# CIN tower with a top MLP: a correction tile over all partitions, top layers by batch halves in three rounded passes, and an earlier first step

## What is computed

```
z   = einsum('bhd,bmd->bhmd', h, x0).reshape(batch, H * M, dim)
out = relu(einsum('bcd,oc->bod', z, W[i]) + b[i])      # i = 0: h = x0;  i = 1: h = the first 64 rows of out
feat = sum over dim of (out0[:, 64:], out1)            # 192 values per sample
h = max([feat, dense_ctx] @ W_top1 + b_top1, 0)        # 208 -> 512
h = max(h @ W_top2 + b_top2, 0)                        # 512 -> 256
y = h @ W_top3
```

## Time and profile before

| | us |
|---|---|
| median of 3 runs (lowest, highest) | 1989.1 (1988.71, 1989.22) |
| profiled execution, its own time | 1987.74 |
| its span | 1985.9 |
| PE busy | 1947.4 (98%) |
| DVE busy | 1912.4 (96%) |
| POOL busy | 1802.8 (91%) |
| ACT busy | 1710.7 (86%) |

### The profile page before, as it was taken

The page is one execution under the profiler, slowest core; times in us unless marked ns, Lnnn a source line. Parts: engine busy times, 40 slices in busy tenths (PEclk is TensorE's granted clock), DMA queues, the critical chain, the costliest instruction groups (busy, mean ns, idle before and its releaser), DMA issues.

```text
span 1985.9 us, 28534 instructions
## 1 busy us (share of the span) xinstructions
PE 1947.4 (98%) x7176; PEld 1340.1 (67%) x7176; DVE 1912.4 (96%) x1231; ACT 1710.7 (86%) x1943; POOL 1802.8 (91%) x708
## 2 busy tenths in 40 slices
PE   3999999999999999999999999999999999999998
PEld 1767766766766766766766666666666666666664
DVE  5999999999999999999999999999999999999991
ACT  4989888888888888888888888888888888888883
POOL 5999999999999999999999999999999999999881
PEclk9999999999999999999999999999999999999999
DMA  8987777777777777777777777777777777777720
GB/s 224 236 203 191 193 182 191 194 184 188 193 185 187 194 186 186 194 187 185 194 188 184 194 189 182 194 190 182 194 191 181 195 192 179 195 192 179 192 63 1
DMA packets 268641, 364.14 MB, mean 183 GB/s; under 512 B 107713, under 2 KB 108097, under 8 KB 268498
## 3 DMA queue, kind: packets, MB, share of 16 engines
q1 hardware_dynamic: 256946, 351.56, 71.9%
q0 software_dynamic: 8192, 8.40, 1.8%
q10 hardware_dynamic: 3488, 4.00, 0.7%
HBM read 347.02 MB, written 16.78 MB: 183 GB/s over the span
## 4 chain that ended last, share of the span: by engine, by line
PE 92%; POOL 5%; issue 2%; DMA 1%; ACT 1%; ACTq 0%; DVE 0%; POOLq 0%
PE out L718 60%; PE out L700 21%; PE out L708 8%; POOL zl L269 5%; PE out L702 1%; PE out L765 0%; PE hrep L765 0%; POOL emb L245 0%; DMA emb<-in_tables,idx 0%; DMA xrep<-fields_dram 0%; DMA fields_dram<-emb 0%; ACT hrep L445 0%; PE out L758 0%; PE z L758 0%; PE hrep L758 0%
## 5 line engine op out<-in xcount | busy, mean ns | idle before, releaser
L269 POOL TENSOR_TENSOR zl<-prod,zh 128x2048 fp32r<-128x2048 f32 (+2 forms) x384 | 1545.6, 4056 | 72.4 <-ACT zh L432 72.4
L718 PE MATMUL out<-zh,w1h 128*128 128x512 f32 x1856 | 754.6, 407 | 1.5 <-ACT relu L438 0.8
L718 PE MATMUL out<-zl,w1h 128*128 128x512 f32 x1856 | 724.4, 390 | 0.0
L718 PE MATMUL out<-zh,w1l 128*128 128x512 f32 x1856 | 723.3, 390 | 0.0
L432 ACT ACTIVATE zh<-prod 128x2048 fp32r<-128x2048 f32 (+2 forms) x384 | 652.7, 1700 | 70.0 <-DVE prod L639 45.3
L445 ACT ACTIVATE hrep<-out,b_sb 32x512 f32<-32x512 f32 (+1 forms) x768 | 495.1, 645 | 84.8 <-PE out L702 75.0
L700 PE MATMUL out<-prod,w_sb 128*128 128x512 f32 x1024 | 464.0, 596 | 31.1 <-DVE prod L574 26.1
L718 PEld LDWEIGHTS out<-zh,w1h 128*128 128x128 f32 x1856 | 348.2, 188 | 170.7 <-POOL zl L269 62.9
L718 PEld LDWEIGHTS out<-zl,w1h 128*128 128x128 f32 x1856 | 348.3, 188 | 75.9
L718 PEld LDWEIGHTS out<-zh,w1l 128*128 128x128 f32 x1856 | 348.8, 188 | 74.5 <-issue 2.6
L700 PEld LDWEIGHTS out<-prod,w_sb 128*128 128x128 f32 x1024 | 194.8, 190 | 228.0 <-issue 218.2
(11 more groups left out here) (64 smaller groups left out, 701.6 us busy)
## 6 DMA issues: line engine op xcount, KB each, us to landing
rot_low<-fields_dram SPq DMA_DIRECT2D x512, 256.0 KB, 6.3
rot_high<-fields_dram SPq DMA_DIRECT2D x512, 256.0 KB, 4.3
xrep<-fields_dram SPq DMA_DIRECT2D x252, 128.0 KB, 2.7
left_y<-fields_dram SPq DMA_DIRECT2D x256, 64.0 KB, 2.2
fields_dram<-emb SPq DMA_DIRECT2D x504, 32.0 KB, 4.6
left_x<-fields_dram SPq DMA_DIRECT2D x252, 64.0 KB, 2.3
emb<-in_tables,idx POOLq DMA_INDIRECT x256, 4.4
w_sb<-in_w ACTq DMA_DIRECT2D x1, 1024.0 KB, 5.2
```

The lines of the kernel that those rows point to most:

```text
L269: pool.tensor_tensor(zl[u][:, 0:size, :], product[:, 0:size, :], zh[u][:, 0:size, :].bitcast(F32), ALU.subtract).then_inc(zl_made[u], 1)
L718: mm = nc.tensor.matmul(out1[:, :], w[:, k, :], z[:, t, :], start=start and t == 0 and part == 0, stop=stop and t == size - 1 and part == 2)
```

## The change

1. **Left part.** A new tile `left_high` has zeros on partitions 0 to 63 (written once). `round_left` rounds only partitions 64 to 127 into it, and `left_low` computes `left_parts = lz - left_high` over all 128 partitions, no longer in place. `round_left` waits for the `left_low` before and no longer for PE; `left_low` now waits for PE (`l0_done`). PE's matmul is the same. In the steps with b = 0, `copy_left` stands behind the rounding of groups 0 and 3 on ACT, and no longer ahead of it.
2. **Top layers.** The order is by batch half, then by tile. Weights, features and the first layer's outputs are split in a rounded part (ACT) and a remainder (DVE), and each fp32 matmul of layers 1 and 2 becomes three fp32r matmuls (`in_three`). The first half's work needs only blocks 0 to 31, so its preparation stands ahead of the last step's results. Layer 2 waits for its inputs tile by tile. Layer 3 stays in fp32. The remainders lie in tiles that the steps no longer use; `w0b_sb` moves into `prod[3]`.
3. **Prologue.** ACT now writes both groups of block 0's second half (SP wrote one), and issues the load of `w1_sb` ahead of its first write. `copy_x(0, 0)`, the second half of `xrep` and `copy_left(0)` stand ahead of the wait for block 1's rows on ACT, and `load_low(1, 1)` ahead of it on SP.

The core of the diff (semaphores and some copies of the same pattern are left out):

```diff
+        left_high = sb("left_high", [P, SC], F32R)
         left_parts = sb("left_parts", [P, SC], F32R)
...
-        w0b_sb = sb("w0b_sb", [P, LOW, OUT])
+        w0b_sb = prod[3][:, 0, :].rearrange("p (a b) -> p a b", b=OUT)
...
+        wt1_parts = [rot_low[0][:, 2 * p:2 * p + 2, :].bitcast(F32R) for p in range(2)]
+        wt2_parts = [rot_low[1][:, 2 * p:2 * p + 2, :].rearrange("p a (b c) -> p (a b) c", c=H2).bitcast(F32R)
+                     for p in range(2)]
+        feat_parts = [(zh[3 + half], zl[3 + half]) for half in range(MN)]
+        h1_parts = [(zh[half], zl[half]) for half in range(MN)]
+        h1_sb = prod[:MN]
+        h2_sb = prod[2:2 + MN]
...
-        banks = [t[:, :] for t in (out0, out1, hrep[0], hrep[1], xr, lz)] + [z4[:, 0, :], z4[:, 1, :]]
+        banks = [t[:, :] for t in (xr, lz, hrep[0], hrep[1])] + [z4[:, 0, :], z4[:, 1, :], out0[:, :], out1[:, :]]
...
+        def sums_relu1(half):
+            first = 1 + half * (BLOCKS // MN)
+            return sums[:, first:first + BLOCKS // MN, SROWS:ENTRY]
...
             write_first(sp, 0, 0, first_written)
-            sp.wait_ge(gathered[0], GATHERED_APART)
-            write_first(sp, 1, 0, scratch_written[0])
             sp.wait_ge(first_written, WRITTEN_APART)
             load_low(0, 0)
             sp.wait_ge(scratch_written[0], written(0, 1))
             load_left(sp, 0, left_y, LEFT, left_y_loaded)
+            load_low(1, 1)
             sp.wait_ge(gathered[1], 16 * GATHERS)
             write_groups(sp, 1, 1, (0, 1))
-            load_low(1, 1)
             load_high(0, 0)
...
             def round_left(n):
                 act.wait_ge(left_made, n + 1)
                 if not known(n) or n > 0:
-                    act.wait_ge(l0_done, n * 2)
-                act.activation(left_parts[:, :], lz[:, :], ACT.Copy).then_inc(left_rounded, 1)
+                    act.wait_ge(left_split, n)
+                act.activation(left_high[HID:P, :], lz[HID:P, :], ACT.Copy).then_inc(left_rounded, 1)
...
                 if not first and is_up_to(i, c, LAST - 2):
                     copy_x(m + 2, b)
+                round_split(m, 0, in_parts(0, b), p1_made, prod[1])
+                round_split(m, 3, in_parts(3, b), z4_made[0], z4)
                 if not first and b == 0 and is_up_to(i, c, LAST - 2):
                     copy_left(i * 2 + (c + 2) // 2)
-                round_split(m, 0, in_parts(0, b), p1_made, prod[1])
-                round_split(m, 3, in_parts(3, b), z4_made[0], z4)
                 if is_past(i, c, 0):
                     finish_l1(m - 1, 1 - b, i * 2 + (c + 1) // 2 - 1)
...
+            act.wait_ge(first_gathered[0], 16)
+            act.dma_start(w1_sb[:, :, :], w1).then_inc(w1_loaded, 16)
             act.wait_ge(first_gathered[1], 16)
             write_first(act, 0, 1, first_written)
-            act.dma_start(w1_sb[:, :, :], w1).then_inc(w1_loaded, 16)
             act.wait_ge(gathered[0], GATHERED_APART)
-            write_first(act, 1, 1, scratch_written[0])
+            for g in range(HGATHERS):
+                write_first(act, 1, g, scratch_written[0])
             act.wait_ge(first_written, WRITTEN_APART)
             load_first_xrep(act, 0, first_xrep_loaded)
             act.wait_ge(scratch_written[0], written(0, 1))
             load_left(act, 0, left_x, 0, left_x_loaded)
+            load_first_xrep(act, 1, xrep_loaded)
+            copy_x(0, 0)
+            copy_left(0)
             act.wait_ge(gathered[1], 16 * GATHERS)
             write_groups(act, 1, 1, (2, 3))
-            copy_x(0, 0)
-            load_first_xrep(act, 1, xrep_loaded)
-            copy_left(0)
             round_left(0)
...
+            def fill_feat0(half):
+                to = feat0[HID:P, half * SC:(half + 1) * SC].rearrange("p (m b r) -> p b m r", b=HALVES, r=SROWS)
+                for b in range(HALVES):
+                    first = half * (BLOCKS // MN) + b
+                    act.activation(to[:, b], sums[b * HID:(b + 1) * HID, first:first + BLOCKS // MN, 0:SROWS],
+                                   ACT.Copy).then_inc(feat0_made, 1)
+            def round_feat0(half):
+                act.wait_ge(feat0_made, (half + 1) * HALVES)
+                act.wait_ge(split_used[3 + half], STEPS)
+                act.activation(feat_parts[half][0][:, 0, :], feat0[:, half * SC:(half + 1) * SC],
+                               ACT.Copy).then_inc(feat_rounded, 1)
+            def round_sums(half):
+                act.activation(feat_parts[half][0][:, 1, :].rearrange("p (n r) -> p n r", r=ROWS), sums_relu1(half),
+                               ACT.Copy).then_inc(feat_rounded, 1)
+            act.wait_ge(top_loaded, 96)
+            act.wait_ge(sums_made, BLOCKS // MN + 1)
+            fill_feat0(0)
+            act.activation(wt1_parts[0], wt1_sb[:, :, :], ACT.Copy).then_inc(wt_rounded, 1)
+            round_feat0(0)
+            round_sums(0)
+            act.activation(wt2_parts[0], wt2_sb[:, :, :], ACT.Copy).then_inc(wt_rounded, 1)
             act.wait_ge(sums_made, BLOCKS + 1)
-            to = feat0[HID:P, :].rearrange("p (m b r) -> p b m r", b=HALVES, r=SROWS)
-            for b in range(HALVES):
+            fill_feat0(1)
             finish_l1(LAST, 1, BLOCKS - 1)
+            round_feat0(1)
...
+            def h1(j):
+                half, c = j // C1, j % C1
                 act.wait_ge(h1_done, j + 1)
-                act.activation(h1_sb[c][:, half, :], banks[j], ACT.Relu, bias=bt1_sb[:, c:c + 1]).then_inc(h1_made, 1)
+                act.activation(h1_sb[half][:, c, :], banks[j], ACT.Relu, bias=bt1_sb[:, c:c + 1]).then_inc(h1_made, 1)
+            def round_h1(j):
+                half, c = j // C1, j % C1
+                act.wait_ge(h1_made, j + 1)
+                if c == 0:
+                    act.wait_ge(split_used[half], STEPS)
+                act.activation(h1_parts[half][0][:, c, :], h1_sb[half][:, c, :], ACT.Copy).then_inc(h1_rounded, 1)
+            h1(0)
+            act.wait_ge(sums_made, BLOCKS + 2)
+            round_sums(1)
+            for j in range(1, C1 * MN):
+                h1(j)
+                round_h1(j - 1)
+            round_h1(C1 * MN - 1)
...
             def left_low(n):
                 dve.wait_ge(left_rounded, n + 1)
-                nc.vector.tensor_tensor(left_parts[HID:P, :], lz[HID:P, :], left_parts[HID:P, :].bitcast(F32),
+                if known(n) and n == 0:
+                    dve.wait_ge(left_zeroed, 1)
+                else:
+                    dve.wait_ge(l0_done, n * 2)
+                nc.vector.tensor_tensor(left_parts[:, :], lz[:, :], left_high[:, :].bitcast(F32),
                                         ALU.subtract).then_inc(left_split, 1)
...
+            def low_weights(k, wt, parts):
+                dve.wait_ge(wt_rounded, k + 1)
+                nc.vector.tensor_tensor(parts[1], wt[:, :, :], parts[0].bitcast(F32), ALU.subtract).then_inc(wt_split, 1)
...
+            def low_h1(j):
+                half, c = j // C1, j % C1
+                high, low = h1_parts[half]
+                dve.wait_ge(h1_rounded, j + 1)
+                nc.vector.tensor_tensor(low[:, c, :], h1_sb[half][:, c, :], high[:, c, :].bitcast(F32),
+                                        ALU.subtract).then_inc(h1_split, 1)
...
+            low_weights(0, wt1_sb, wt1_parts)
+            low_feat0(0)
+            low_sums(0)
+            low_weights(1, wt2_sb, wt2_parts)
             dve.wait_ge(relu1_made, STEPS)
             sum_rows(BLOCKS, slice(0, P), slice(1, 1 + HALVES))
+            low_feat0(1)
+            low_sums(1)
+            for j in range(C1 * MN):
+                low_h1(j)
...
+            def in_three(out, w, z, first, last):
+                for part, (wp, zp) in enumerate(((w[0], z[0]), (w[1], z[0]), (w[0], z[1]))):
+                    mm = nc.tensor.matmul(out, wp, zp, start=first and part == 0, stop=last and part == 2)
+                return mm
...
+            pe.wait_ge(wt_split, 1)
+            for half in range(MN):
+                pe.wait_ge(feat_split, 2 * (half + 1))
+                for c in range(C1):
+                    j = half * C1 + c
+                    if banks[j] is out1:
+                        pe.wait_ge(relu1_made, STEPS)
+                    for k in range(2):
+                        mm = in_three(banks[j], [w[:, k, c * P:(c + 1) * P] for w in wt1_parts],
+                                      [z[:, k, :] for z in feat_parts[half]], k == 0, k == 1)
                     mm.then_inc(h1_done, 1)
-            pe.wait_ge(h1_made, C1 * MN)
-            for c in range(C2):
-                for half in range(MN):
+            pe.wait_ge(wt_split, 2)
+            for half in range(MN):
+                for c in range(C2):
+                    j = half * C2 + c
                     for k in range(C1):
-                        mm = nc.tensor.matmul(banks[c * MN + half], wt2_sb[:, k, c * P:(c + 1) * P],
```

(17 more changed lines are left out.)

31 lines of the change are left out of this document (19 added, 12 removed).

## The result

| us | before | after |
|---|---|---|
| median (lowest, highest), 4 runs each, same chip | 1989.02 (1988.71, 1989.22) | 1972.51 (1972.13, 1972.92) |
| profiled execution: its own time, its span | 1987.74, 1985.9 | 1972.53, 1970.7 |

The ratio is 0.9916, with a 95% interval of [0.9903, 0.9928]: 16.5 us faster. The forecast was 1970.5, so the result is 2.0 us above it and inside the range of 1966 to 1978.

What follows compares the result with a forecast made beforehand. DVE was taken to bound the kernel from about 270 us, hidden behind PE's 98% busy. Gains 6.9 + 9.85 + 0.4 + 1.5 = 18.65 cut the span from 1985.9 to 1967.3, giving a median of 1970.5; range 1966 to 1978.

Steps and rivals of the forecast that it cites:

- Part 1, forecast 6.9: Left part in the steady steps: 57 pairs fall to PE's 29.734 us each, gaining 6.9 us; bounds 0 and 9.7.
- the chain's two paces: PE's pairs of steps: 29.734 us each up to 242.56 us, PE's own need; 29.867 from 272.38, set by DVE.
- the three held intervals: DVE starts around `left_low`, once a pair: 0.11, 0.12 and 0.14 us too long, together 0.37, all closed by the change.
- the cut at PE's own pace: DVE would need 29.50 us a pair, but PE needs 29.734, so the gain is only 0.133 a pair.
- The rival that DVE stays the bound: Steady steps: the intervals have another cause and stay; gain only 11.3 us, 1977.8 in all; chance 0.11.
- `copy_left`, forecast 0: ACT, steps with b = 0: moving it behind two roundings costs 0, hidden by a 0.6 us margin before POOL needs `zh`.
- The rival that rounding would be late for POOL: `copy_left` delays `zh` of group 1; each 0.1 us beyond the margin costs 6.3, with 0.4 more 1996; chance 0.04.
- Part 2, forecast 9.85: Top layers: three passes at 0.229 us a matmul without PE waits, 25.59 us against 35.44; bounds 7 to 10.
- Three passes bring nothing: Top layers: matmuls on reused tiles run at fp32's 0.446 us; layers 1 and 2 take 21.4 each, total 1991; chance 0.02.
- The last step, forecast 0.4: Last step, where PE waits for POOL: DVE's lead lets POOL start earlier, gaining 0.4 us; bounds 0 and 0.7.
- Part 3, forecast +1.5: Prologue: first copy at 21.1 us, first `hrep` at 30.9 instead of 32.38, gaining 1.5; bounds -0.5 and 3.0.
- the prologue gives back: Prologue: writes and loads collide, first `hrep` no earlier, 1972.0; chance 0.09 for prologue or top layers falling short.

Runs made afterwards that it cites:

- run 5: The kernel before with one line changed: `left_low` in place on partitions 0 to 127, output not the reference's; 1980.93 us, ratio 0.9961.
- run 6: The kernel before with one line changed: `left_low` in place on partitions 0 to 63, output not the reference's; 1982.34 us, ratio 0.9964.
- run 1: The kernel before with only the left part changed, including the place of `copy_left`; 1981.13 us, ratio 0.9959.
- run 12: The changed kernel with `copy_left` back ahead of the rounding of groups 0 and 3 in steps with b = 0; 1974.04 us, ratio 0.9922.
- run 4: The changed kernel with the prologue of before; 1971.09 us, ratio 0.9909 to before.
- run 9: The changed kernel with block 0's second-half writes shared by SP and ACT again and the `w1_sb` load back behind the first write; 1969.47 us, ratio 0.9899.
- run 11: The changed kernel with SP's 1 MB `load_low(0, 0)` issued behind its wait for block 0's written rows; 1971.90 us, ratio 0.9912.
- run 7: The changed kernel with only the load of `w1_sb` put back behind the first write; 1973.92 us, ratio 0.9925.
- run 10: run 9 with the load of `w1_sb` issued only behind the second half of `xrep`; 1971.52 us, ratio 0.9909 to before.
- run 3: The kernel before with only the prologue changed; 1993.06 us, ratio 1.0018.
- run 2: The kernel before with only the top layers changed; 1979.32 us, ratio 0.9948.

## Why the prediction came out as it did

**Part 1, forecast 6.9, measured 6.56.** The reading of the chain's two paces, the bound on DVE, the three held intervals and the cut at PE's own pace were right. Runs 5 and 6 settle the cause. PE's own pace was taken as 29.734 and is 29.740, which makes 0.3 over 57 pairs. The rival that DVE stays the bound fell in run 1. One of the signs named was wrong: DVE's idle time of 0.11 us in the pair doesn't show as a wait of DVE; what shows are waits of ACT for PE.

**`copy_left`, forecast 0.** Right for the margin in the steady state, which is what was argued, and wrong as a sum: the first steps, where its rows land late, weren't looked at. The move is worth 1.2 us there (run 12). The rival that rounding would be late for POOL did not occur; the margin of 0.6 held.

**Part 2, forecast 9.85, measured 10.12** (25.32 us against 25.59 forecast). The pace of 0.229 us for a matmul holds on the reused tiles (it is 0.227: 96 of them in 21.76 us, 1943.15 to 1964.91), and PE doesn't wait once. ACT's preparations are eight instructions, as in the sum, though the list of the change counts seven; they were done at 1939.8, and the last relu waited 3.36 us for PE. Layer 3's own part is 3.56 in place of 3.63. "Three passes bring nothing" fell.

**The last step, forecast 0.4, measured 0.38, for another reason.** Between the last group and the last step lie four more pairs, 118.96 us against 119.54, a gain of 0.58 which the forecast hadn't counted. The last step alone got 0.16 longer (24.93 against 24.77, from layer 0's last matmul to the end of the split matmuls). So DVE's lead was worth nothing there.

**Part 3, forecast +1.5, measured -1.84.** This is the step that failed, beyond its bound of -0.5 (by run 4 and after, -1.6), and the sign that was named for it, a first copy after 22 us, came: 24.98. What stands behind the time of block 0's rows was right: in run 9, with the rows at 15.93, the first copy came at 21.37 (forecast 21.1) and the first `hrep` at 30.03 (30.9). The wrong step was the sentence that ACT's two more writes come first, "but `w1_sb` starts earlier and is out of their way", which put the rows at 16.3 with 17.2 as the bound; they were written at 19.97. Three things were missed in it:
- The early load of `w1_sb` is not out of the way but in the way of the gather ahead: 2.5 us.
- Taking a write from SP moves forward all that SP issues next. That is 1 MB, and it got ahead of the writes (3.2 us of the 5.2, run 11). Only `left_x` was looked at for that, not the writes.
- SP's stream is then 3.5 us late for block 2 as well, and ACT waits 1.15 and 2.74 us for `xrep` in steps 0 and 2. The forecast ended at the first `hrep`, where nothing was lost (0.05), and took it for the start of all that follows.

The rival "the prologue gives back" had the right direction, with 1972.0; but it took no gain for its worst case, and the loss went on by 1.8.

**The median.** Part of the miss was covered by a constant: the forecast's span was 1967.3, and the real one 3.4 above it. The median was taken 1.4 above the profiled execution, as before the change; after it they were equal (1972.51 and 1972.53). So the final number is only 2.0 off, and the 1.4 were luck: in 15 other executions the kernel before ran from 1987.19 to 1991.31, and its profiled one, 1987.74, lies at the low end.

## What to carry to other kernels

An engine at 96% with no waits can be the bound of one at 98%: look for the place where the pace in the chain changes, and then for start-to-start intervals on the other engine that are longer than elsewhere for the same shape. A VectorE instruction on partitions 64 to 127 can cost more than a full one: here 0.37 us a pair, at its neighbours.

Where a DMA issue is taken off a queue, ask what that queue issues next and whether this gets in front of the transfer that others wait for; and follow a change in a prologue until the steady pace begins, not to its first result. Two copies of one prologue can differ by 0.8 us at that point, so a smaller effect needs its own rows and not only the span.

## What was unexpected of the hardware

- A write of 32 KB took 2.0 us with no load of 1 MB issued in the 7 us ahead of it, 5.2 with 1 MB issued 1.7 us earlier on the other engine's queue, and 7.7 with loads of 1 MB issued 1.7 and 3.2 us earlier (runs 11, after, 7).
- A gather that was issued 0.7 us behind a 1 MB load landed 2.5 us later than without it. The same load took 10.6 us when issued among other loads (run 10), against 5.2 before.
- PE's idle time of 2.12 us ahead of the top layers was followed by two to three rows at the lower clock in runs 5 and 6, and not in before, 1 or 3. What decides between them stays open.
- The same eight matmul records at the start of PE's work took from 5.13 us (after) to 6.46 us (run 2). What sets that is open.
- Open as well: why `xrep` for step 2 took 12.5 us in run 9 and 10.2 before, at the same busy share of the DMA engines.
